# Row transposes behind the last product of a block, and the copies that stack u ahead of a weight load

## What is computed

```
h = shift_token(x)                       # upper half of the columns comes from the row before
h = (h - mu) / sqrt(var + 1e-5) * lg + lb
h = h @ w1 + b1                          # 512 -> 2 x 1365
a, g = split(h, 2)
h = a * gelu(g)
x = x + h @ w2 + b2                      # 1365 -> 512
```

## Time and profile before

| | |
|---|---|
| median of 3 runs | 2930.35 us |
| the profiled execution's own time | 2932.76 us |
| its span, first to last instruction | 2930.9 us |
| granted TensorE clock, mean | 0.998 |
| TensorE busy (matmul / weight load) | 98% / 86% |
| VectorE, ScalarE, GpSimd busy | 71%, 46%, 46% |
| transfers | 547.01 MB, mean 187 GB/s |

### The profile page before, as it was taken

How to read it: one execution, slowest core, us unless ns; L and a number is a source line. 1 busy time by engine, 2 the same in 40 slices (tenths; PEclk the granted TensorE clock), 3 DMA queues, 4 the chain that set the end, 5 groups by cost and what they waited for, 6 DMA issues and landing times. The chain is left out here.

```text
span 2930.9 us, 53002 instructions
## 1 busy us (share of the span) xinstructions
PE 2884.4 (98%) x20256; PEld 2531.0 (86%) x20256; DVE 2075.9 (71%) x4135; ACT 1341.3 (46%) x2807; POOL 1337.9 (46%) x1406
## 2 busy tenths in 40 slices
PE   9999999999999999999999999999999999999999
PEld 7887888888889899999998887878888899999998
DVE  8977777777667666766657768777666766666765
ACT  7865656555553222222235555556564322222222
POOL 7757677776542211122205667776662222212221
PEclk9999999999999999999999999999999999999999
DMA  6753233322157677776683223332127677777775
GB/s 219 238 184 98 94 113 104 109 91 80 37 199 276 252 266 265 266 259 256 255 314 110 94 98 109 106 111 93 57 76 282 241 279 270 273 277 275 276 276 188
DMA packets 184480, 547.01 MB, mean 187 GB/s; under 512 B 26262, under 2 KB 82074, under 8 KB 161700
## 3 DMA queue, kind: packets, MB, share of 16 engines
q1 hardware_dynamic: 184084, 543.56, 52.1%
q10 hardware_dynamic: 144, 0.07, 0.0%
HBM read 447.11 MB, written 93.70 MB: 185 GB/s over the span
## 5 line engine op out<-in xcount | busy, mean ns | idle before, releaser
L1242 PE MATMUL quad<-fhT_f,slot_f 128*128 128x256 f32 (+1 forms) x2088 | 596.4, 286 | 0.2 <-DVE sums_f L2056 0.2
L1243 PE MATMUL quad<-fhT_f,slot_f 128*128 128x256 f32 (+1 forms) x2088 | 590.2, 283 | 0.0
L1244 PE MATMUL quad<-fhT_f,slot_f 128*128 128x256 f32 (+1 forms) x2088 | 589.9, 283 | 0.0
L1242 PEld LDWEIGHTS quad<-fhT_f,slot_f 128*128 128x128 f32 (+1 forms) x2088 | 392.7, 188 | 1.4 <-DVE sums_f L2056 0.8
L1243 PEld LDWEIGHTS quad<-fhT_f,slot_f 128*128 128x128 f32 (+1 forms) x2088 | 392.9, 188 | 0.0
L1244 PEld LDWEIGHTS quad<-fhT_f,slot_f 128*128 128x128 f32 (+1 forms) x2088 | 392.9, 188 | 0.0
L1661 ACT ACTIVATE gate_f_raw<-gate_f_raw,bias_f 128x512 f32<-128x512 f32 (+1 forms) x176 | 127.2, 722 | 576.9 <-DVE gate_f_raw L2079 576.9
L1529 ACT ACTIVATE lprob<-lprob,small 128x384 f32<-128x384 f32 (+2 forms) x512 | 288.5, 565 | 179.1 <-DVE small L1880 179.1
L2164 POOL TENSOR_SCALAR stats<-stats 128x1 f32<-128x1 f32 x64 | 43.5, 680 | 707.5 <-DVE stats L2019 706.8
L2281 POOL TENSOR_TENSOR turned_qk<-with_cos,with_sin 128x256 f32<-128x256 f32 x252 | 186.9, 763 | 337.0 <-DVE with_sin L1904 243.6
L996 PE MATMUL bank_pair<-wqkv_h,hT 128*128 128x512 f32 x992 | 318.6, 402 | 0.0
(11 more groups left out here) (296 smaller groups left out, 7349.4 us busy)
## 6 DMA issues: line engine op xcount, KB each, us to landing
slot_f<-parts SPq DMA_DIRECT2D x160, 1792.0 KB, 7.6
slot_f<-parts SPq DMA_DIRECT2D x16, 1190.0 KB, 5.2
s_in<-stream SPq DMA_DIRECT2D x128, 128.0 KB, 2.7
s_res<-stream SPq DMA_DIRECT2D x64, 256.0 KB, 2.8
stream<-a_out SPq DMA_DIRECT2D x64, 256.0 KB, 2.0
res_f<-stream SPq DMA_DIRECT2D x63, 256.0 KB, 7.3
h_in_f<-stream SPq DMA_DIRECT2D x112, 128.0 KB, 6.7
parts<-part_high SPq DMA_DIRECT2D x20, 512.0 KB, 2.6
```

Source lines behind the costliest of these rows:

```text
L1242: e.matmul(bank[0:n, :], high, row_high, start=c == 0, stop=False)
L1243: e.matmul(bank[0:n, :], high, row_low, start=False, stop=False)
L1244: ins = e.matmul(bank[0:n, :], low, row_high, start=False, stop=c == 1)
```

## The change

On TensorE `turn_normalised` is written behind `up_third`, so that the transposes follow the seventh product of their block and not the fifth. On SyncE `stack_u(g - 1)` is written ahead of the slot load in block (g, 0). Every wait, transfer and matmul stays what it was. `turn_first_rows`, which stands in the same place of the code, is still ahead of `up_third`.

```
             for g in range(GROUPS):
                 for j in range(HC):
+                    if g and j == 0:
+                        stack_u(g - 1)
                     if 3 <= g * HC + j + 2 < BLOCKS:
                         load_slot(l, g * HC + j + 2)
                     if g == 0 and 6 <= j + 5 < HC:
                         load_down(l, j + 5)
-                    if g and j == 0:
-                        stack_u(g - 1)
                     if g and j == 2:
                         finish_group(g - 1)
...
                     up_first(l, g, j)
                     up_second(l, g, j)
+                    if l + 1 < DEPTH and (g, j) == (GROUPS - 1, 9):
+                        turn_first_rows(l + 1)
+                    up_third(l, g, j)
                     if g + 1 < GROUPS and j in (2, 4, 6, 8):
                         w.wait_ge(S("s1"), step + g * HC + j + 1)
                         turn_normalised(l, (g + 1) * GROUP + j // 2 - 1)
-                    if l + 1 < DEPTH and (g, j) == (GROUPS - 1, 9):
-                        turn_first_rows(l + 1)
-                    up_third(l, g, j)
```

## The result

The changed kernel takes 2938.03 us (median of 18 runs, 2935.07 to 2942.37), the kernel before took 2932.14 beside it (18 runs, 2930.16 to 2933.91). The ratio is 1.0020, with a 95% interval from 1.0013 to 1.0027: 5.9 us slower. The forecast was 2922, 8 us faster, with a range up to 2937. The profiled execution took 2935.61 us with a span of 2933.8.

What follows compares the result with a forecast made beforehand. TensorE, busy 2884.4 of 2930.9 us, was taken as the bound, leaving its waits and low clock. Gains of 13.7 and 12.5 less 18.2 of slot waits made 8.0 us: 2930.35 to 2922, range 2908 to 2937.

Steps and rivals of the forecast that it cites:

- X: Time from the issue of the copies of u to the slot load's landing at (g, 2): taken as 11.6 us.
- The long waits go: Stacked matmuls (line 1311): copies issued first land long before use, ending two waits of 3.27 and 3.80 us.
- Edit 1, 13.7 us: Transposes moved behind the seventh product: 14 waits on ScalarE's copy of the first product vanish, 13.7 us gained.
- worry (b): `down(g, 0)` may wait for `finish_group`'s four adds, up to 0.25 us each, at most 2.5 us.
- 12.5 less 2 x 1.9: First groups: 7.4 us of long waits and 5.1 of low clock gained, less slot waits of 11.6 - 9.7 in two places.
- X = 2.3 + (4.2 to 5.4) + 4.6: Slot load behind the copies: start and finish, copies' hold of their queue, load's share in it; 11.1 to 12.3 us.
- the like order: `stack_weights` with a load behind: 12.8 us from copies' issue to landing, 12.1 less the 256 KB load between.
- 14 x 12.0 - 144.2: Slot waits of TensorE over 14 places, from the forecast's formula 14 X - 144.2.
- 26.2: Gain forecast from the moved transposes and the removed long waits with their low clock, before the slot waits' cost.
- The third rival: Late slot load takes exactly what the moved transposes gave: X about 12 to 12.6, within 5.9 us of 2930; 25%.
- The waits of 1.2 us leave the clock as it is: TensorE's clock at the new slot waits: not lowered, as after none of the 14 waits of 0.8 us.
- the first rival: Slot load at (g, 2) lands in time, X at or under 10.2: gain 22.7 us, 2908 us; 10%.

Runs made afterwards that it cites:

- edit 1 alone: Only the transposes moved behind `up_third`, SyncE's order as before, against the kernel before: 2924.29 us, ratio 0.9973.
- the split copies: Changed kernel with the 43-row copies of u and of the weights each issued as 32 and 11 rows: 2915.11 us, ratio 0.9944 to the kernel before.
- Edit 2 alone: Only `stack_u` moved ahead of the slot load on SyncE, transposes as before, against the kernel before: 2939.56 us, ratio 1.0025.

## Why the forecast was wrong, step by step

Two steps of the prediction failed. The copies' hold on their engine, in the sum for X, was too small. And the landing of the copies themselves was priced at nothing ("The long waits go"). The mechanism of the rest was right.

**Edit 1, 13.7 us.** Right in the changed kernel: 13.6 us, 13.3 of them in the 14 places, with no wait left. The worry (b) about VectorE's adds came true with edit 1 alone, 2.9 us for the 2.5 forecast, and not in the changed kernel, where the blocks start late, as the prediction had it. Not in the sum: the first `down` matmul behind transposes is some 0.03 us late each time, in 40 places or so, 1.0 us in all.

**"With nothing ahead they land long before their use at 1046.8. The long waits go."** This half failed. The copies land 7.4 to 8.1 us behind their issue with nothing ahead of them. In later groups that is in time (use at 8.5), but in layer one's first group the use without a wait is at 7.1 (line 1311 with the split copies), and TensorE waits 0.81 us there and 1.30 in layer two's. Then the slot is late as well. Of the 8.7 us that the two first groups were to give net (12.5 less 2 x 1.9), 3.2 came: 5.5 us missing. Of these 2.1 are the two waits and 1.7 the stretch at 0.50 in layer two; the remaining 1.7 is not told apart. I had taken the slot load's landing as the only thing to come late and did not price the landing of the copies themselves.

**"X = 2.3 + (4.2 to 5.4) + 4.6"; "I take 11.6".** The mechanism was right: all 14 places wait for the slot, and the load lands 9.9 to 10.7 us behind its issue. The size was off. X is 12.0 in the mean (11.5 to 12.2). Its parts as the packets of the changed kernel show them, means over the 14 places: 1.3 us from issue to first packet, 5.8 for the copies on their engine (43 packets and three of the 42-row copy), 4.5 for eight packets of the slot load that follow on it without a gap (0.7 us and seven times 0.54), 0.5 to its landing, 12.0 with rounding. Against the prediction's terms: start and finish 1.8 and not 2.3, the load's share 4.5 for 4.6, and the hold of the copies 5.8 (5.3 to 6.0) and not 4.2 to 5.4. The hold was read as the distance of two landings, the load's and the copies', but in (2, 0) of the kernel before the copies' packets had started on that engine at 1040.4, 1.4 us before the load's landing at 1041.8. My shading, "towards the lower one, since the queue is empty when the copies come", was without ground; the reading from the like order, `stack_weights` with a load behind, gave 12.1 and was right. The error has a large lever: fourteen times 0.4 us is 5.6. In the twelve places it came to 19.8 where 14.4 was forecast, 5.4 more. Yet with X at 12.0 the prediction's own sum still makes the kernel 2.4 us faster (14 x 12.0 - 144.2 = 23.8 against 26.2); only with the second failed step does it become slower.

**The third rival,** X from 12 to 12.6 and the whole "within 5.9 us of 2930", is what came about, with X at its lower edge and the time at its upper. It had 25%, since the chances hung on X too.

**The clock.** "The waits of 1.2 us leave the clock as it is": in the profiled execution that held in thirteen of the fourteen places, behind waits of 1.92 and 1.94 us too, and not in the last first group. Edit 2 alone showed 0.50 for 3.4 us at 960.6, 1226.9 and 2503.4, behind waits of up to 1.9. So some stretches at 0.50 came with the new waits, and I had priced none.

Together: -8.0 forecast, + 5.4 + 5.5 + 1.0 from these steps and -1.2 in the attention phases gives + 2.7, against + 2.9 in the traces. The 3 us between the traces and the medians (+ 5.9) are the part that is only argued.

The Trainium skill, "DMA: Bandwidth & Descriptors", section "Why a DMA increments its semaphore by 16 and not by 1", lets the number of engines be the largest number up to 16 that divides the slowest dimension of both sides, here the count of rows: one for 43, sixteen for 32, eleven for 11. The runs agree: 43 rows in one DMA or in two halves are one row of packets, and the copies of 32, 11 and 42 rows land at 3.8 us in ten of the 14 places of the changed order. The table "Specifications" of the same page of the Trainium skill gives an engine about 27 GiB/s, by which, as an estimate, these 86 KB pass in 3.0 us. They took 4.65 us in the best case, and here the measurement decides: the first rival, which this figure spoke for, was wrong by its price.

## What to carry to other kernels

Look at a small transfer's rows before looking at its place in the queue: here 86 KB held one DMA engine for 5 to 6 us, the 1792 KB behind them landed 1.7 us later than behind the same rows split, and order only decided who paid. Before one transfer is moved ahead of another, take the time for which the issuing engine was free as what it is, a head start that the wait in front now swallows. And where a price is multiplied by the number of places, take the nearest like case as it stands, and price the landing of what is moved as well as of what it passes.

## What the runs showed of the hardware

- Two queues on one DMA engine took turns packet by packet, without regard to the packets' sizes: 2 KB packets beside 14 KB ones went at one per 0.62 to 0.68 us, where alone they take 0.084, and an 86 KB copy took 20.2 to 21.4 us to land in place of 7.4 to 8.1. In one queue they were served in order.
- On one engine, 86 packets of 1 KB took 4.65 to 4.76 us and 43 of 2 KB 4.9 to 5.6, at the same place of the kernel: smaller packets did no harm, and the kernel gained 11.5 us.
- An engine may be through with a transfer well before the transfer has landed: in (2, 0) of the kernel before, the copies' packets began on their engine 1.4 us before the landing of the load ahead of them.
- Issuing three DMAs in place of two took SyncE 0.6 to 0.75 us longer (2.08 and 2.22 against 1.47).
